# Second cross-attention of a two-layer Perceiver: three chunks of split operands and three score banks in place of two

## The reference

```
Sim  = (xn @ w1)[:, None] + (ctx @ w2)[None, :] + (xn * w3) @ ctx.T + b     # 128 x 12544
A    = softmax(Sim, axis=1);          hat = A @ ctx                          # 128 x 256
Batt = softmax(max(Sim, axis=1));     bar = Batt @ xn                        # 1 x 256
y    = concat(xn, hat, xn * hat, xn * bar) @ W_qv + b_qv;    x = x + y
```

## Time and profile before

| | us |
|---|---|
| median of 3 runs (lowest, highest) | 953.68 (953.63, 955.01) |
| profiled execution, its own time | 953.95 |
| span of its trace, first to last instruction | 952.2 |
| the loop of this stage on PE, from `score(0)` to the first matmul of `sums(24)` | 703.77 to 799.39 |

### The profile page before, as it was taken

The page is one execution under the profiler, slowest core; times in us unless marked ns, Lnnn a source line. Parts: engine busy times, 40 slices in busy tenths (PEclk is TensorE's granted clock), DMA queues, the critical chain, the costliest instruction groups (busy, mean ns, idle before and its releaser), DMA issues.

```text
span 952.2 us, 30588 instructions
## 1 busy us (share of the span) xinstructions
PE 923.3 (97%) x13329; PEld 722.8 (76%) x13329; DVE 693.9 (73%) x872; ACT 574.6 (60%) x1408; POOL 373.3 (39%) x406
## 2 busy tenths in 40 slices
PE   7999999999999999999999999969989999999998
PEld 5677777777777777776667777758978787899998
DVE  4588888888888888788888888865036554368887
ACT  5666666666666666676666666624146663346764
POOL 2644444444444444444444444300123331513332
PEclk9999999999999999999999999989999999999999
DMA  6011101110110110000011000039758988409992
GB/s 238 24 26 26 26 25 25 26 25 25 25 25 25 25 25 25 25 25 25 25 25 26 19 9 3 3 128 397 256 194 273 283 274 275 170 2 319 324 333 92
DMA packets 78554, 98.10 MB, mean 103 GB/s; under 512 B 21584, under 2 KB 56928, under 8 KB 78432
## 3 DMA queue, kind: packets, MB, share of 16 engines
q1 hardware_dynamic: 77344, 94.67, 30.9%
q10 hardware_dynamic: 1088, 1.57, 0.5%
HBM read 95.68 MB, written 0.13 MB: 101 GB/s over the span
## 4 chain that ended last, share of the span: by engine, by line
PE 94%; DVE 3%; ACT 1%; DMA 1%; issue 0%; POOL 0%; ACTq 0%; DVEq 0%
PE ps L370 29%; PE ps L421 18%; PE ps L431 9%; PE ps L379 7%; PE ps L1594 6%; PE ps L1169 4%; PE ps L1071 3%; PE ps L1611 2%; PE ps L1615 2%; PE ps L1612 2%; PE ps L1158 2%; PE ps L287 1%; PE ps L1160 1%; PE ps L1159 1%; PE ps L1176 1%; PE ps L1417 1%
## 5 line engine op out<-in xcount | busy, mean ns | idle before, releaser
L681 DVE TENSOR_REDUCE x_peak<-ps 128x2 f32<-128x1024 f32 (+1 forms) x200 | 240.3, 1205 | 96.4 <-PE ps L421 87.7
L597 ACT ACTIVATE probs<-ps,x_peak 128x512 f32<-128x512 f32 (+1 forms) x400 | 266.2, 683 | 54.3 <-DVE x_peak L681 53.7
L700 DVE STREAM_TRANSPOSE probsT<-probs 128x1024 f32<-128x1024 f32 (+1 forms) x200 | 225.5, 1182 | 2.8 <-ACT probs L597 2.8
L421 PE MATMUL ps<-keys,qT 64*32 64x512 f32 (+1 forms) x3200 | 224.0, 585 | 1.4 <-ACT keys L584 0.6
L584 ACT COPY keys<-ps 128x512 f32<-128x512 f32 (+1 forms) x200 | 113.8, 583 | 144.1 <-PE ps L370 144.1
L431 PEld LDWEIGHTS ps<-probsT,vals 64*32 64x32 f32 x6016 | 116.8, 106 | 78.0 <-issue 73.3
L869 POOL TENSOR_SCALAR vals<-vals_t,x_side 128x512 f32<-128x512 f32 (+1 forms) x100 | 152.2, 1541 | 51.3 <-PEq L439 51.3
L370 PE MATMUL ps<-ctxT_hi,wk_hi 128*128 128x512 f32 (+1 forms) x400 | 157.4, 393 | 0.2 <-DVE wk_lo L734 0.2
L370 PE MATMUL ps<-ctxT_lo,wk_hi 128*128 128x512 f32 (+1 forms) x400 | 154.2, 385 | 0.0
L370 PE MATMUL ps<-ctxT_hi,wk_lo 128*128 128x512 f32 (+1 forms) x400 | 154.1, 385 | 0.0
L431 PE MATMUL ps<-probsT,vals 64*32 64x128 f32 x6016 | 131.5, 270 | 0.4 <-issue 0.4
(11 more groups left out here) (259 smaller groups left out, 1297.6 us busy)
## 6 DMA issues: line engine op xcount, KB each, us to landing
m_w<-in_m_w SPq DMA_DIRECT2D x32, 1024.0 KB, 7.6
ctx_raw<-in_ctxT SPq DMA_DIRECT2D x24, 512.0 KB, 3.7
ctx_two<-in_ctxT SPq DMA_DIRECT2D x24, 512.0 KB, 4.0
ctx_one<-in_ctx SPq DMA_DIRECT2D x24, 512.0 KB, 5.1
x_shrinkT<-x_shrink SPq DMA_DIRECT2D x384, 1.0 KB, 1.7
f_h1T<-in_f_h1T SPq DMA_DIRECT2D x1, 4096.0 KB, 18.5
f_h2T<-in_f_h2T SPq DMA_DIRECT2D x1, 4096.0 KB, 28.2
m_shared_w<-in_m_sw SPq DMA_DIRECT2D x2, 1024.0 KB, 7.4
```

What stands on the lines that cost most here:

```text
L421: i = pe.matmul(m.ps[32 * j:32 * (j + 1), score_bank(t) + odd, 0:nt * P], m.qT[rows, 4 * group + j, qs], m.keys[rows, 4 * group + j, 0:nt ...
L597: return act.activation(m.probs[t][:, odd, 0:nt * P], m.ps[:, score_bank(t) + odd, 0:nt * P], ACT.Exp, bias=m.peak[slot][:, 1, 2 * (t // H ...
L681: dv.tensor_reduce(m.peak[slot][:, 1, cs, t % HALF], m.ps[:, bank:bank + 2, 0:nt * P], AX.X, ALU.min).then_inc(s["dve" if t == STEPS - 1 e ...
L700: i = dv.transpose(m.probsT[:, cs, 0:4 * nt, t % HALF * 32:t % HALF * 32 + 32], m.probs[t][:, :, 0:nt * P].rearrange("p c (b k) -> p c b k ...
```

## The change

```diff
+    behind_parts, m.at = m.at, base + 32 * KIB
+    m.c1_hi.append(m.new("c1T_hi2", [DK, CHUNK], F32R))
+    m.c1_lo.append(m.new("c1T_lo2", [DK, CHUNK], F32R))
...
+X1_BANKS, AHEAD = (0, 1, 6), 3
...
-        dst = m.bank(c % 2)[:, cols]
+        dst = m.bank(X1_BANKS[c % AHEAD])[:, cols]
...
     pe.wait_ge(s["x1_init"], 1)
+    score(1)
     for c in range(N_FULL + 1):
-        if c + 1 <= N_FULL:
-            score(c + 1)
+        if c + 2 <= N_FULL:
+            score(c + 2)
         if c >= 1:
             sums(c - 1)
```

In `xattn1_scalar`:

```diff
     residual_kept(act, m, s, m.x[1][:, :], 0, 4)
+    high(2)
     act.wait_ge(s["x1_g_ready"], 1)
...
     for c in range(N_FULL + 1):
-        if c + 2 <= N_FULL:
-            high(c + 2)
         if c + 1 <= N_FULL:
             probabilities(c + 1)
+        if c + AHEAD <= N_FULL:
+            high(c + AHEAD)
         keep_turned(c)
```

In `xattn1_vector`:

```diff
+    low(2)
     dv.wait_ge(s["x1_init"], 1)
     maximum(0)
     for c in range(N_FULL + 1):
-        if c + 2 <= N_FULL:
-            low(c + 2)
         if c + 1 <= N_FULL:
             maximum(c + 1)
+        if c + AHEAD <= N_FULL:
+            low(c + AHEAD)
...
         if c >= 1:
             add_sums(c - 1)
```

More of the change, by code:

```diff
@@ L208, in place @@
     m.c1_lo = [m.new(f"c1T_lo{i}", [DK, CHUNK], F32R) for i in range(2)]
+    behind_parts, m.at = m.at, base + 32 * KIB
+    m.c1_hi.append(m.new("c1T_hi2", [DK, CHUNK], F32R))
+    m.c1_lo.append(m.new("c1T_lo2", [DK, CHUNK], F32R))
+    assert m.at <= mid
+    m.at = behind_parts
     m.pr = [m.new(f"x1_pr{i}", [CHUNK]) for i in range(2)]
@@ L1155, in score @@
         pe.wait_ge(s["x1_split1"], c + 1)
-        dst = m.bank(c % 2)[:, cols]
+        dst = m.bank(X1_BANKS[c % AHEAD])[:, cols]
         for k in range(DK):
-            pe.matmul(dst, m.gT_hi[:, k, :], m.c1_hi[c % 2][:, k, cols], start=(k == 0), stop=False)
-            pe.matmul(dst, m.gT_hi[:, k, :], m.c1_lo[c % 2][:, k, cols], start=False, stop=False)
-            t = pe.matmul(dst, m.gT_lo[:, k, :], m.c1_hi[c % 2][:, k, cols], start=False, stop=(k == DK - 1))
+            pe.matmul(dst, m.gT_hi[:, k, :], m.c1_hi[c % AHEAD][:, k, cols], start=(k == 0), stop=False)
+            pe.matmul(dst, m.gT_hi[:, k, :], m.c1_lo[c % AHEAD][:, k, cols], start=False, stop=False)
+            t = pe.matmul(dst, m.gT_lo[:, k, :], m.c1_hi[c % AHEAD][:, k, cols], start=False, stop=(k == DK - 1))
         t.then_inc(s["x1_scores_full"], 1)
@@ L1231, in high @@
         act.wait_ge(s[f"turned{c % RING}"], 16 * (c // RING + 1))
-        act.copy(m.c1_hi[c % 2][:, 0, cols], m.ctx_two[c % RING][:, 0, cols]).then_inc(s["x1_hi0"], 1)
-        act.copy(m.c1_hi[c % 2][:, 1, cols], m.ctx_two[c % RING][:, 1, cols]).then_inc(s["x1_hi1"], 1)
+        act.copy(m.c1_hi[c % AHEAD][:, 0, cols], m.ctx_two[c % RING][:, 0, cols]).then_inc(s["x1_hi0"], 1)
+        act.copy(m.c1_hi[c % AHEAD][:, 1, cols], m.ctx_two[c % RING][:, 1, cols]).then_inc(s["x1_hi1"], 1)
     def probabilities(c):
@@ L1237, in probabilities @@
         act.wait_ge(s["x1_max_kept"], c + 1)
-        act.activation(m.pr[c % 2][:, cols], m.bank(c % 2)[:, cols], ACT.Exp,
+        act.activation(m.pr[c % 2][:, cols], m.bank(X1_BANKS[c % AHEAD])[:, cols], ACT.Exp,
                        bias=m.negm1[:, new:new + 1], scale=1.0).then_inc(s["x1_pr_ready"], 1)
@@ L1276, in low @@
         dv.wait_ge(s["x1_hi0"], c + 1)
-        dv.tensor_tensor(m.c1_lo[c % 2][:, 0, cols], m.ctx_two[c % RING][:, 0, cols], m.c1_hi[c % 2][:, 0, cols],
+        dv.tensor_tensor(m.c1_lo[c % AHEAD][:, 0, cols], m.ctx_two[c % RING][:, 0, cols], m.c1_hi[c % AHEAD][:, 0, cols],
                          ALU.subtract).then_inc(s["x1_split0"], 1)
@@ L1282, in maximum @@
         dv.wait_ge(s["x1_scores_full"], c + 1)
-        dv.tensor_reduce(m.negc1[:, new:new + 1], m.bank(c % 2)[:, 0:tiles(c) * P],
+        dv.tensor_reduce(m.negc1[:, new:new + 1], m.bank(X1_BANKS[c % AHEAD])[:, 0:tiles(c) * P],
                          AX.X, ALU.max).then_inc(s["dve"], 1)
@@ L1350, in low @@
         gp.wait_ge(s["x1_hi1"], c + 1)
-        gp.tensor_tensor(m.c1_lo[c % 2][:, 1, cols], m.ctx_two[c % RING][:, 1, cols], m.c1_hi[c % 2][:, 1, cols],
+        gp.tensor_tensor(m.c1_lo[c % AHEAD][:, 1, cols], m.ctx_two[c % RING][:, 1, cols], m.c1_hi[c % AHEAD][:, 1, cols],
                          ALU.subtract).then_inc(s["x1_split1"], 1)
```

## The result

The changed kernel takes 963.23 us (median of 5 runs, 962.61 to 964.45), the kernel before 953.68 (median of 5, 952.67 to 955.96). The ratio is 1.0093, 95% interval [1.0078, 1.0109]: slower by 0.9%, about 9 us. The medians and ratios in this document leave out three runs that stood far above all others of their kernel (1043.56 us with the maxima in PSUM and the start filled, 1045.71 and 1885.77 us with the kernel before).

The account below looks back on a forecast made before the run. The kernel was taken as bound by waits over ACT, POOL and DVE, 3.77 us a turn, PE close behind. `sums(23)` 7.7 us later: 953.95 + 7.7 = 961.65, less 0.27 to the median, 961.4; range 959.4 to 963.5 (74%).

Parts of the forecast that it names:

- The ring before: Loop of the kernel before: a closed path of waits over ACT, POOL, DVE and ACT sets the turn, 3.77 us.
- TensorE's own pace: Same loop: the turn PE could keep without waiting, 3.6 us; as a rival bound after the change, chance 8%.
- The stall of `negm1`: DVE's small operation stands until POOL finishes, 0.52 us against 0.16; forecast to return to 0.16 after the change.
- The new ring: Changed loop: score, sums, add, reduction, `negm1`, exponential, copies, POOL, score; 8.20 us over two turns, 4.10 a turn.
- The loads cost nothing: Slot reloads, wanted by ACT one turn sooner, still have over 6 us and land in 4.0, so no cost.
- The add is not held by POOL: DVE's add of the sums keeps its usual length, 0.47 us, though POOL runs; nothing was added for it.
- This rival: DVE's add is held by POOL's port: 4.58 us a turn, about 970 us in all; chance 8%.
- the two others: Period set through the transposes, 3.85 us a turn, 956.3 (6%); or by PE, 3.6, 951.4 or 952.6 (8%).
- the one through the transposes: Path from transposes by ACT's copy and exponential to score: 7.69 us over two turns, 956.3 in all; chance 6%.
- The start: First turns of the stage: PE's first stall partly filled, score of turn 1 at 710.91, of turn 2 at 714.22.
- Alternating turns: Weight loads of `score` in the loop: 4.10 us apart, perhaps 4.02 and 4.19 in turns.
- The end: From `score(24)` to `sums(23)`: 7.52 us against 4.51 before, as a whole turn without a score lies between.

## Why the prediction was right

961.4 was forecast and 963.23 measured, slower as forecast, near the upper end of the range of 959.4 to 963.5. By the prediction's own steps:

- *The ring before, 3.77 us.* Right. Its links were shown by taking one out: with `negm1` no longer held, the turn is 3.57; with the ring restored it is 3.78. TensorE's own pace, taken as 3.6, is 3.57.
- *The stall of `negm1` goes.* Right, 0.16 in place of 0.52.
- *The new ring, 8.20 over two turns.* Right to 0.01 us. `score(4)` to `score(24)`: 797.70 − 715.64 = 82.06 for the 82.0 forecast. That it is this ring is shown by its cut (add later: 7.71), its stretching (reduction twice: 8.80), and the version in which ScalarE doesn't close it (3.57 a turn).
- *The loads cost nothing.* Right: no copy of the changed kernel waits for one. The cover was thin, as waits of 0.17 to 0.78 us in three of the other versions show.
- *The add is not held by POOL.* Right, 0.48 throughout. This rival falls, as do the two others in the changed kernel itself. The rings that they were made of are real, though: the one through the transposes came up when the add was moved, TensorE's pace when the copies were.
- *The start.* This is the term of the sum that was mis-sized. `score(4)` was forecast for 714.22 in a stage whose `score(0)` begins at 703.77. It came at 715.64 with `score(0)` at 703.32, so 1.87 later. I had counted TensorE at the full clock there; two stretches near 1.2 GHz put its products 0.43 apart in place of 0.23. With TensorE kept busy the clock stayed up and 1.91 us came back.
- *Alternating turns.* 4.02 and 4.19 were forecast; 3.59 and 4.61 came. Their sum is given by the ring, their split by the start: with the start filled they are 4.00 and 4.22.
- *The end.* 7.52 from `score(24)` to `sums(23)`, measured 805.33 − 797.70 = 7.63.

Together: `sums(23)` came at 805.33 against 796.05, 9.3 later, of which 1.87 − 0.45 + 0.06 + 0.11 = 1.6 beyond the 7.7 that were forecast (start, earlier begin of the stage, ring, end). That the stage began 0.45 earlier is luck: no step of the prediction has it, and it hides part of the error of the start. All behind it moved along: 9.2 in the span.

What is wrong in the change is then one thing. The new order on VectorE is worth its while, as it frees `negm1` from POOL. The one on ScalarE closes the ring and costs 13 us against 950.2. Both versions faster than the kernel before get there by freeing `negm1`, and their ratios, 0.9951 and 0.9957, can't be told apart; the one with the maxima in PSUM needs neither a third set nor a new order. Whether VectorE's new order would do as well with two sets, with ScalarE's copies left first, was not run.

## What to carry to other kernels

Before two operations of an in-order engine are swapped, write down for both what they wait for and who waits for them, and follow every closed path; its length divided by the turns that it spans is a floor for the period, and deeper buffers help only the paths that cross them. Here the third set gave 3.3 us at the start of the loop and took 3.1 at its end. A "100% busy" TensorE may still be paced by another engine: look at what ends the idle time of the weight load. And a tiny operation that ends exactly when another engine's ends, and takes three times its usual time, is probably held by it, which moving one of its operands can test; the place of one operand was worth as much here as the best reordering.

## What the runs showed of the hardware

- TensorE's granted clock fell in some profiles and not in others for nearly the same order of work. In the kernel before TensorE was idle for 1.79 us ahead of `score(0)`, where it waited for the low part of `gT`, and for 1.88 us ahead of `score(2)`, and the clock stayed at 1.00. With the maxima in PSUM the same two waits were as long, and from 708 to 712 the clock was 0.57. In the changed kernel the two falls came behind 1.79 us of idle (ahead of `score(0)`) and 2.08 us (709.30 to 711.37). In the three profiles with the start filled it stayed at 1.00 there. What decides isn't settled here. The falls also differ between executions of one kernel: over a whole run the mean granted clock was 0.992 to 0.995 with the changed kernel, 0.991 to 0.996 with the kernel before, and 0.995 or 0.996 with the filled versions.
- The lower clock cost 1.9 us in the changed kernel, some 10 us with the new orders alone, and 1.1 us or less within the stage in the two faster versions, nothing that the time shows.
- A VectorE operation whose scalar comes from SBUF, with one tensor in PSUM and one in SBUF, is not held by POOL: 0.48 in all 25 adds of the changed kernel, ten of them wholly inside a POOL instruction. With two tensors in SBUF `negm1` is held (0.52 for 0.16).
- The products of the scores, with operands that the kernel declares as `fp32r`, are 0.23 us apart at 512 columns; those of the sums, with operands declared as `f32`, are 0.22 apart at 257 columns. Per column `fp32r` takes about half as long here.
